# Layer-1 attention: ScalarE rounds k directly behind q, and the exponential of the second key tile comes third

## The reference

```
xn = layer_norm(x, gamma, beta)
q, k, v = heads(xn @ Wq), heads(xn @ Wk), heads(xn @ Wv)
att = einsum('bhid,bhjd->bhij', q, k) / 64 ** 0.5 + alibi_bias
out = einsum('bhij,bhjd->bhid', softmax(att), v) @ Wo
```

## Time and profile before

| | |
|---|---|
| median of 3 runs | 3428.2 us (3427.2 to 3432.61) |
| profiled execution: its own time | 3427.71 us |
| its span, first to last instruction | 3425.9 us |
| mean granted TensorE clock | 0.923 of full speed |
| TensorE busy | 2955.4 us (86%) |
| VectorE, GpSimd, ScalarE busy | 2152.8, 1737.6, 1523.4 us |

### The profile page before, as it was taken

How to read it: one execution, slowest core, us unless ns; L and a number is a source line. 1 busy time by engine, 2 the same in 40 slices (tenths; PEclk the granted TensorE clock), 3 DMA queues, 4 the chain that set the end, 5 groups by cost and what they waited for, 6 DMA issues and landing times.

```text
span 3425.9 us, 43451 instructions
## 1 busy us (share of the span) xinstructions
PE 2955.4 (86%) x13360; PEld 1893.8 (55%) x13360; DVE 2152.8 (63%) x3692; ACT 1523.4 (44%) x1974; POOL 1737.6 (51%) x954
## 2 busy tenths in 40 slices
PE   4799999788779999978877999997887799999787
PEld 3555555566545555556655555555665455555565
DVE  5556666477555666647745666665774556666577
ACT  1245555255225555535522555553552355554354
POOL 2045555477205555547710555564770155556476
PEclk7899999899879999989977999998997899999799
DMA  3000000010100000000010000000101000000100
GB/s 134 2 7 7 9 7 7 17 37 28 46 2 9 7 9 7 6 27 28 28 46 3 8 8 8 9 3 27 37 18 46 3 8 9 7 9 4 36 28 24
DMA packets 23389, 65.54 MB, mean 19 GB/s; under 512 B 3796, under 2 KB 13012, under 8 KB 23128
## 3 DMA queue, kind: packets, MB, share of 16 engines
q1 hardware_dynamic: 23288, 64.24, 5.7%
HBM read 62.10 MB, written 4.22 MB: 19 GB/s over the span
## 4 chain that ended last, share of the span: by engine, by line
PE 68%; DVE 13%; issue 9%; ACT 6%; POOL 2%; DMA 0%; DVEq 0%; ACTq 0%; SPq 0%; POOLq 0%
PE P L1276 13%; PE P L1239 9%; PE P L1264 6%; PE P L1261 6%; PE P L1361 4%; PE P L1220 4%; PE P L1362 3%; PE P L1363 3%; PE P L1226 3%; DVE Kb L789 2%; PE P L1340 2%; DVE mhalf L793 2%; PE P L1163 2%; ACT Ka L921 2%; PE P L1284 2%
## 5 line engine op out<-in xcount | busy, mean ns | idle before, releaser
L793 DVE TENSOR_REDUCE mhalf<-P 128x1 f32<-128x512 f32 x1024 | 664.4, 686 | 316.6 <-PE P L1226 183.5
L949 ACT ACTIVATE pfull<-P 128x1024 f32<-128x1024 f32 x512 | 523.7, 1023 | 635.9 <-PE P L1264 632.3
L447 POOL TENSOR_TENSOR opair<-opair,pfull 128x1024 f32<-128x1024 f32 x192 | 455.6, 2373 | 164.1 <-ACT pfull L949 163.5
L447 POOL TENSOR_TENSOR spair<-spair,pfull 128x1024 f32<-128x1024 f32 x192 | 458.5, 2388 | 145.9 <-ACT pfull L949 141.8
L1276 PE MATMUL P<-pfull,V 128*64 128x512 f32 x2048 | 495.0, 605 | 0.0
L1239 PE MATMUL P<-Ka,Qa 96*128 96x512 f32 x1024 | 417.9, 462 | 83.3 <-DVE Kb L789 39.7
L1361 PE MATMUL P<-Kb,R 128*128 128x512 f32 x864 | 379.9, 440 | 126.8 <-DVE Qb L834 125.3
L1261 PE MATMUL P<-Qa,Ka 98*128 98x512 f32 x1024 | 451.6, 441 | 5.4 <-ACT Qa L938 4.4
L1264 PE MATMUL P<-Qb,Kb 128*128 128x512 f32 x1024 | 433.7, 424 | 0.0
L834 DVE TENSOR_TENSOR Qb<-A,Kb 128x512 fp32r<-128x512 f32 x288 | 302.0, 1048 | 172.0 <-ACT Kb L1025 172.0
L1239 PEld LDWEIGHTS P<-Ka,Qa 96*128 96x128 f32 x1024 | 192.4, 192 | 324.4 <-DVE mhalf L793 243.9
(11 more groups left out here) (205 smaller groups left out, 4334.5 us busy)
## 6 DMA issues: line engine op xcount, KB each, us to landing
wex<-in_wex SPq DMA_DIRECT2D x40, 768.0 KB, 4.2
Ka<-auxrows SPq DMA_DIRECT2D x64, 128.0 KB, 2.2
wpair<-in_whead SPq DMA_DIRECT2D x64, 96.0 KB, 2.0
modb<-modrows SPq DMA_DIRECT2D x4, 768.0 KB, 6.3
A<-in_x SPq DMA_DIRECT2D x5, 512.0 KB, 3.4
x<-in_x SPq DMA_DIRECT2D x4, 512.0 KB, 3.3
out_x<-x SPq DMA_DIRECT2D x4, 512.0 KB, 2.7
A<-in_consts SPq DMA_DIRECT2D x1, 1872.0 KB, 15.5
```

Of the source, the lines that this page charges most:

```text
L447: pool.tensor_tensor(psum8[s][:, :], psum8[s][:, :], pfull[:, j % RING, :], ALU.add).then_inc(S["p_added"], 1)
L793: dve.tensor_reduce(mhalf[:, i, t:t + 1], P[:, 6 + i, :], AX.X, ALU.max, negate=True).then_inc(S["max_red"], 1)
L949: act.activation(pfull[:, j % RING, :], banks(2 * (j % 2)), ACT.Exp, scale=DH1 ** -0.5).then_inc(S["exp_done"], 1)
```

## The change

In ScalarE's program `k_high` moves from behind the exponential of key tile 1 to directly behind `q_high`. The exponential of tile 1 is so the third of the group, and `outputs` of the previous head stays fourth. It applies to all 15 switches of a batch. No instruction is added, removed or resized, no semaphore wait is changed, and the other engines' programs stay as they are.

```
                         if ahead and jj == 0:
                             q_high(1 - s, n + 1)
+                            k_high(1 - s, n + 1)
                         if ahead and jj == T - 1:
                             maxima(1 - s, n + 1)
                             if s == 1:
...
                             exps(k + 1, jj + 1, n)
                         elif ahead:
                             exps(k + 1, 0, n + 1)
-                        if ahead and jj == 0:
-                            k_high(1 - s, n + 1)
                         if behind and jj == 0:
                             outputs(1 - s, n - 1)
```

## The result

The changed kernel takes 3401.3 us (median of 6 runs, 3399.6 to 3405.9), the kernel before 3428.3 in the same series: ratio 0.9922, 95% interval [0.9909, 0.9935], 27.0 us faster. The forecast was 3408 with a range of 3398 to 3419: the result lies inside the range, some 7 us under the forecast. The profiled execution took 3400.61 us against 3427.71, so 27.1 us less; its span is 3398.8 us.

A forecast was written before the change was run, and what follows sets the result against it. TensorE was taken to set the pace, with only its stops at head switches worth anything. Per batch 6 x 0.32 + 6 x 0.41 + 3 x 0.25 = 5.1 us, four batches 20.5, gave 3408 us, range 3398 to 3419.

The forecast's parts named there:

- The path: At the head switches of the attention, TensorE idles for k_lo, 39.7 us in 60 places: the most to be gained.
- e1 pays for it: At an odd-head switch, tile 1's exponential ends 0.85 us later, delaying tile 3's scores; weighing still comes 0.32 us earlier.
- The rest of the head moves up with it: Behind each switch, row-maxima reductions and exponentials start earlier too; no engine holds the head's end in place; cost nothing.
- k_high beside q_lo costs nothing: At the switches both read PSUM banks 6 and 7 at once, keeping 1.02 and 1.22 us; cost nothing.
- Time = before less 20.5: Whole execution: 3427.7 - 20.5 = 3407.2 us profiled, said as 3408 for the median; chance 0.58.
- (B): Outside the attention, granted clock takes or gives up to 10 us; chance 0.27 for 3412 to 3420, 0.03 under 3400.
- Rival (D): At the switches, overlapped reads by k_high and q_lo disturb each other; some 53 us lost, 3481 us; chance 0.06.

The follow-up runs named there:

- k_apart: The changed kernel, but k_high also waits until q_lo is done, so ScalarE and VectorE don't read banks 6 and 7 together; 3537.9 us, ratio 1.0309.

## Why the prediction was right, and where it was off

- The path: TensorE's stops, ended by k_lo. Right; the 39.7 us went from that wait in full.
- e1 pays for it, and the stop moves to the scores of tile 3. Right, to 0.01 us: 0.32 us per odd head. In even heads 0.36 instead of 0.41: the scores took 1.31 us to the start of max_tile after the stop, where I took 0.97 + 0.28, and the weighing followed 0.68 us behind. The last switch of a batch gave 0.20 us and the first two 0.19 and 0.20 from head to head, where I had put 0.25 for each. The sum of the attention came to 19.5 us instead of 20.5.
- The rest of the head moves up with it. Right: the row maxima's wait is 280.9 us, 280.4 before.
- k_high beside q_lo costs nothing. Right, 60 times over. "Advanced Engine Details and Errata", section "Bank Collisions", of the Trainium skill speaks of the same bank within the same partition; this trace agrees, with 1.02 and 1.22 us for two readers on different partitions of the same banks.
- "Time = before less 20.5" was the step that failed in size. The stages behind the attention were taken to shift by 5.1 us per batch, with (B) as a symmetric scatter of 10 us around that. Repeating batches don't scatter: they come out 3.4 us apart, so four of them could give 4 x 3.4 = 13.7 or 4 x 6.8 = 27.3 us, and 20.5 lies between. 27 us is what was measured. By the attention alone the time would have been 3428.3 - 19.5 = 3408.8; it is the 7.6 us outside it that brought 3401.3, in the direction that (B) called luck, to whose far end, under 3400, I had given a chance of 0.03. The result lies in the range because (B) had put the lower end at 3398; that part was luck. That the three batch lengths of before lay within 0.2 us of each other was to be seen in the trace, and I did not use it.
- Rival (D), which did not come true, had its price wrong: 110 us, not 53, since with the longer stop TensorE was also at 1.2 GHz for 27 us more per attention.

What is shown: the steps, by one trace of each of fourteen kernels whose batch lengths, from the second batch on, are 836.3, 839.7, 843.1, 846.5 us and, in k_apart, 873.8, eight steps above 846.5, all within 0.1 us or so; and that work added to a batch can cost nothing or a whole step. What is only argued: that the granted clock is the carrier. The time at 1.2 GHz goes with the length of the stretch in twelve kernels, and in the two with the experts' dose the made-up time lies where the clock is higher; but that is going together, and no run held the clock still to see whether the steps vanish. Which place decides on the step is open too: a dose in the experts was absorbed where one of half that size in the attention was not.

## What to carry to other kernels

When an engine's in-order program holds two consumers of different urgency, price the swap by what waits for the one that is put back: here 1.02 us earlier for k_low cost 0.85 us of the exponential, and 0.3 to 0.4 us of the whole was left; in the attention it gained more to give TensorE other ready work for the moved stop (5.8 us per batch against 4.9). A kernel whose loop repeats to a tenth of a microsecond while its granted clock changes inside may be held to steps: read the loop's length in two kernels before adding small gains up, and don't judge a change of a few tenths of a per cent by one comparison, since it may show as nothing or as twice its size.

## What the runs showed of the hardware that was not expected

A program of four batches on one core, with a mean granted clock of 0.923, so at 1.2 GHz for some 15% of the time, had batch lengths, from the second batch on, only in steps of 3.4 us. TensorE work of 0.86 us per batch cost 3.4 us per batch; the next 2.6 us were free; 1.7 us were free in another kernel. And with a stop of TensorE of 2.13 us in odd heads of an otherwise busy stage, the clock fell in some of them (mean 0.90 to 0.95 over the head); with stops of up to 0.9 us, in the other kernels, no head of the third batch behind the first 30 us of the attention was seen below 1.00.
